# A decoder layer on one core: multiplications of a zero tile placed ahead of TensorE's waits in the first two bodies

## The reference: what is computed

```
x = layernorm(x + linear_attention(x))          # q, k = gelu(xW+b)+0.21, rotary; kv = k^T v per head, 16 heads of 8
x = layernorm(x + cross_attention(x, ctx))      # 77 context rows, softmax over them, output projection
x = layernorm(x + mixture_of_experts(x))        # 16 experts 128->256->128, top 4 of 16, all experts computed
```

## Time and profile before

| | before |
|---|---|
| runs | 711.3, 711.61, 710.29 us |
| median | 711.3 us |
| the profiled execution: its time | 711.3 us |
| the profiled execution: its span, first to last instruction | 709.5 us |
| PE busy | 640.7 us (90%), 6772 matmuls |
| VectorE, ScalarE, GpSimd busy | 433.1, 340.4, 107.8 us |
| mean granted TensorE clock | 0.991 |

### The profile page before, as it was taken

The page is one execution under the profiler, slowest core; times in us unless marked ns, Lnnn a source line. Parts: engine busy times, 40 slices in busy tenths (PEclk is TensorE's granted clock), DMA queues, the critical chain, the costliest instruction groups (busy, mean ns, idle before and its releaser), DMA issues.

```text
span 709.5 us, 17624 instructions
## 1 busy us (share of the span) xinstructions
PE 640.7 (90%) x6772; PEld 496.5 (70%) x6772; DVE 433.1 (61%) x1425; ACT 340.4 (48%) x439; POOL 107.8 (15%) x99
## 2 busy tenths in 40 slices
PE   1655886899999999999999999999999989999994
PEld 0433772678867887788778877887778766777773
DVE  0355455757588667867686758675876666356434
ACT  1511314276437643574438543864367435843440
POOL 6540200031002200221013000410032100000000
PEclk9999999999999999999999999999999999999998
DMA  7511001000010001010101000000100010000000
GB/s 195 153 31 46 18 11 37 18 3 27 16 39 18 18 15 47 2 30 9 37 18 30 9 24 28 17 24 12 40 17 0 4 34 4 17 1 1 16 1 16
DMA packets 27152, 19.17 MB, mean 27 GB/s; under 512 B 4568, under 2 KB 24776, under 8 KB 27112
## 3 DMA queue, kind: packets, MB, share of 16 engines
q1 hardware_dynamic: 22952, 13.39, 7.0%
q10 hardware_dynamic: 3872, 4.81, 2.2%
q0 software_dynamic: 288, 0.42, 0.2%
HBM read 8.85 MB, written 2.10 MB: 15 GB/s over the span
## 4 chain that ended last, share of the span: by engine, by line
PE 67%; issue 9%; SPq 9%; DVE 8%; ACT 2%; ACTq 2%; DMA 1%; POOL 1%; DVEq 0%; POOLq 0%
PE ps L792 25%; PE ps L743 9%; SPq L296 8%; PE ps L782 6%; PE ps L784 6%; PE ps L783 6%; PE ps L610 2%; DVE mx L985 2%; PE ps L635 1%; PE ps L624 1%; PE ps L706 1%; ACTq L454 1%; DMA q_rep<-zero_rows 1%; PE ps L629 1%; PE ps L720 1%
## 5 line engine op out<-in xcount | busy, mean ns | idle before, releaser
L792 PEld LDWEIGHTS ps<-w,g 128*128 128x128 f32 x2048 | 244.3, 192 | 25.2 <-issue 11.9
L792 PE MATMUL ps<-w,g 128*128 128x128 f32 x2048 | 256.0, 278 | 3.4 <-DVE acc L1086 3.2
L549 ACT ACTIVATE g<-ps,b 128x512 f32<-128x512 f32 x256 | 167.2, 685 | 162.5 <-PE ps L784 161.6
L1086 DVE SCALAR_TENSOR_TENSOR acc<-ps,cw,acc 128x128 f32<-128x128 f32 x448 | 126.1, 344 | 139.5 <-PE ps L792 139.4
L782 PE MATMUL ps<-x2h,w1h 128*128 128x512 f16 x256 | 98.0, 383 | 1.2 <-DVE x2l L1010 1.0
L784 PE MATMUL ps<-x2h,w1l 128*128 128x512 f16 x256 | 97.5, 381 | 0.0
L783 PE MATMUL ps<-x2l,w1h 128*128 128x512 f16 x256 | 97.5, 381 | 0.0
L374 POOL TENSOR_TENSOR rstd<-ve,half_pow 128x4 f32<-128x4 f32 x32 | 32.7, 1022 | 282.8 <-DVE ve L869 282.8
L524 ACT ACTIVATE w_stage<-ps 77x2048 f32<-77x2048 f32 x32 | 60.0, 1874 | 23.1 <-PE ps L720 22.9
L985 DVE TENSOR_REDUCE mx<-ps 128x8 f32<-128x616 f32 x64 | 49.0, 794 | 8.5 <-PE ps L706 7.5
L393 POOL TENSOR_TENSOR qr<-q_cos,q_sin 128x512 f32<-128x512 f32 x8 | 13.6, 1705 | 224.4 <-DVE q_sin L902 185.8
(11 more groups left out here) (146 smaller groups left out, 707.2 us busy)
## 6 DMA issues: line engine op xcount, KB each, us to landing
q_rep<-qx SPq DMA_DIRECT2D x96, 32.0 KB
x<-in_x SPq DMA_DIRECT2D x8, 256.0 KB, 2.9
w_stage<-in_L_ffn_w ACTq DMA_DIRECT2D x1, 2048.0 KB, 19.4
q_swap<-q SPq DMA_DIRECT2D x16, 128.0 KB, 2.0
out<-fin SPq DMA_DIRECT2D x8, 256.0 KB, 2.3
k_rep<-kx SPq DMA_DIRECT2D x96, 19.2 KB
cx<-in_ctx SPq DMA_DIRECT2D x8, 154.0 KB
cst<-constants ACTq DMA_DIRECT2D x1, 328.5 KB, 9.1
```

The source lines that it names most:

```text
L549: act.activation(g32[:, e % RING, h, :], bH[:, h, :], ACT.Gelu, bias=b1[:, e, h:h + 1], scale=1.0 / WS).then_inc(s["gelu"], 1)
L792: m = pe.matmul(bY[:, b * P:(b + 1) * P], g32[:, e % RING, h, b * P:(b + 1) * P], w2[:, e, h, :], start=(h == 0), stop=(h == HALF - 1))
L1086: m = dve.scalar_tensor_tensor(out=(acc_all if e == E - 1 else acc)[:, b, :], in0=bY[:, b * P:(b + 1) * P], scalar=cw[:, b, e:e + 1], in1= ...
```

## The change

A tile `idle` of zeros (128x512, f16) is added; VectorE writes it as its first instruction, and a semaphore `i_idle` tells PE. PE then issues 16 products of 128x128 by 128x512 of this tile into `bH` before its first real wait, and in the first two bodies `fill(name)` issues more of them ahead of the waits of the operations named in `FILL_FIRST` and `FILL_EARLY`. Each entry is a pair: so many long ones (512 columns) and so many short ones (128 columns). The results are never read. In all there are 66 long and 119 short ones. `filler` is empty from the third body on, and nothing else is changed.

```diff
+FILL_START = 16
+FILL_FIRST = dict(q=(14, 0), kv01=(0, 8), kv23=(0, 9), k_mean=(0, 12), kv=(4, 6), den=(0, 8), out=(0, 3), v1=(0, 5), k=(12, 0),
+                  x1_t=(4, 4), q_x=(0, 7))
+FILL_EARLY = dict(q=(0, 8), kv01=(0, 8), kv23=(0, 9), scores=(7, 0), max_t=(3, 3), kv=(0, 4), den=(0, 2), out=(0, 3), values=(0, 3),
+                  wo=(0, 5), q_x=(0, 7), x2_t=(6, 0), v1=(0, 5))
...
+        idle = sb("idle", [P, T], F16)
...
+            filler = {}
+
+            def fill(step):
+
+                long, short = filler.get(step, (0, 0))
+                for _ in range(long):
+                    pe.matmul(bH[:, 0, :], idle[:, 0:P], idle[:, :], start=True, stop=True)
+                for _ in range(short):
+                    pe.matmul(bH[:, 0, 0:P], idle[:, 0:P], idle[:, 0:P], start=True, stop=True)
+
+            pe.wait_ge(s["i_idle"], 1)
+            for _ in range(FILL_START):
+                pe.matmul(bH[:, 0, :], idle[:, 0:P], idle[:, :], start=True, stop=True)
             pe.wait_ge(s["ld_id"], 16)
...
                 if p == at["q"]:
+                    fill("q")
                     pe.wait_ge(s["i_wtc"], 2)
...
             def body(f, g, a):
-                nonlocal at
+                nonlocal at, filler
                 at = PE_EARLY if f is None else PE_AT
+                filler = {} if f is not None else FILL_EARLY if g is not None else FILL_FIRST
...
             at = DVE_EARLY
+            dve.memset(idle[:, :], 0.0).then_inc(s["i_idle"], 1)
```

More of the change, by code:

```diff
@@ L227, in build @@
         names = """ld_id ld_c ld_b1 ld_wide ld_xwide ld_xw ld_b ld_in ld_w1 ld_w2 ld_x ld_cx ld_swap ld_rep ld_mx st_out
-            i_ones i_idb i_rows i_wt i_wtc i_b1t i_b2 i_wh i_ws i_wl i_rw i_rwl i_v1 i_lg
+            i_ones i_idle i_idb i_rows i_wt i_wtc i_b1t i_b2 i_wh i_ws i_wl i_rw i_rwl i_v1 i_lg
             x_tp x_tc q_p qg q q_cos q_sin qr kv01_p kv23_p kb v kg k_cos k_sin kr
@@ L604, in linear @@
                     if p == at[("kv01", "kv23")[j]]:
+                        fill(("kv01", "kv23")[j])
                         if j == 0:
@@ L613, in linear @@
                 if p == at["k_mean"]:
+                    fill("k_mean")
                     since(pe, "kg", a + 1)
@@ L620, in linear @@
                 if p == at["kv"]:
+                    fill("kv")
                     since(pe, "kr", a + 1)
@@ L626, in linear @@
                 if p == at["den"]:
+                    fill("den")
                     since(pe, "kv", a + 1)
@@ L631, in linear @@
                 if p == at["out"]:
+                    fill("out")
                     since(pe, "den", a + 1)
@@ L647, in entry @@
                 if p == at["v1"]:
+                    fill("v1")
                     since(pe, "cx_tc", a + 1)
@@ L653, in entry @@
                 if p == at["x1_t"]:
+                    fill("x1_t")
                     since(pe, "x1", a + 1)
@@ L659, in entry @@
                 if p == at["k"]:
+                    fill("k")
                     since(pe, "v1", a + 1)
@@ L663, in entry @@
                 if p == at["q_x"]:
+                    fill("q_x")
                     since(pe, "x1_tc", a + 1)
@@ L669, in cross @@
                 if p == at["max_t"]:
+                    fill("max_t")
                     since(pe, "mxl", g + 1)
@@ L684, in cross @@
                 if p == at["wo"]:
+                    fill("wo")
                     since(pe, "ao", 2 * (g + 1))
@@ L689, in cross @@
                 if p == at["x2_t"]:
+                    fill("x2_t")
                     since(pe, "x2n", g + 1)
@@ L695, in scores @@
             def scores(g, b, half):
+                if b == 0 and half == 0:
+                    fill("scores")
                 if b == 0:
@@ L728, in values @@
                 M = 4 * HD
+                if b == 0:
+                    fill("values")
                 since(pe, "prob", n + 1)
```

## The result

| | before | after |
|---|---|---|
| runs | 710.29 to 711.74 us (4) | 718.9, 725.07, 722.55, 718.42 us |
| median | 711.45 us | 720.72 us |
| the profiled execution: time, span | 711.3, 709.5 us | 718.9, 717.1 us |
| instructions, all engines | 17624 | 17995 |
| mean granted TensorE clock | 0.991 | 0.951 |

The ratio is 1.0138, interval 1.0097 to 1.018. The change is slower, on the other side of the forecast and outside its range. The 371 further instructions are 185 products of two instructions each on PE (a weight load and a matmul) and the memset. The two mean clocks can't be held against each other: the kernel before shows 1.00 for its first 100 us, in which its products run at the low level, while the changed kernel shows its low stretches there (0.50 from 16 to 20 us).

A forecast was written before the change was run, and what follows sets the result against it. The chain of waits up to the second `kx` was taken as the bound, PE only after a second series of issues. Terms 3.1 + 1.0 + 0 + 1.0 = 5.1 us gave 711.3 - 5.1 = 706.2 us; 8-in-10 range 699.5 to 711.0.

The forecast's parts named there:

- whatever it gains up to there moves all that is behind it: Up to the second `kx`, at 107.02 us before: any gain there was taken to move everything later by as much.
- the slower side: Whole kernel slower by over 1.4 us, chance 0.07, given to fillers that last longer than the waits they stand in.
- The fillers' sum, 5.1 us: Total gain claimed: 3.1 first body, 1.0 second body's products, 0 values, 1.0 tail.
- `kg` 0.5 us earlier: First body, up to the gelu of k: gain 0.5 us, limited by ACT converting DMA-fed weights until 25.34 us.
- L624, L629, L635: 2.9, capped at 3.1 by POOL: First body: faster products gain 1.0 + 0.9 + 1.0, 3.4 us with the earlier 0.5, but POOL allows 3.1 at most.
- the rival of a fall before `kv`: First body: clock already falls before `kv`, L624, L629 and L635 stay slow; gain 1.5 us, 709.8 us, chance 0.18.
- L662 and scores low: L662 and the second body's scores come at the low clock level after long idle waits; no gain from either.
- Second body 1.0, values 0, tail 1.0: Gains taken from possible ranges: second body's products 0 to 2.8 us, values 0 to 7.0, tail 0 to 1.9.
- the first rival: Clock holds through the second body's values: gain 15.4 us, 695.9 us, or 700 with two fast; chance 0.20, some or all.
- Short filler 0.107 us, load nothing: Each short filler streams 0.107 us at the low level, 0.053 at the high; its weight load was taken as hidden.
- fillers outlast the waits: First two bodies: fillers finish after their waits and delay products, 712.1 to 714.2 us; chance 0.12 including no effect.
- that rival's streaming part: Streaming alone of fillers longer than their waits costs 0.8 us in all, second body's short waits counted.

The follow-up runs named there:

- pad_185: The kernel before with 185 one-column products at PE's start, the same 370 added instructions: 723.85 us against 711.29, ratio 1.0175.
- fill_pad_71: The changed kernel with all its fillers plus 71 one-column products at PE's start, a shift of 512 instructions: 710.86 us, ratio 0.9997 to the kernel before.
- more_fill: The changed kernel with longer fillers, more waits filled (values b=2 too) and 16 one-column products at the start, shift 512: 702.66 us against 712.1, ratio 0.9866.
- early_only: The changed kernel with only the start and second-body fillers, plus 39 one-column products, shift 256: 710.52 us, ratio 0.9976 to the kernel before.
- pad_2: The kernel before with 2 one-column products, a shift of 4 instructions: 718.38 us, one run.

## Why the prediction was wrong

**The step that failed** is in the first paragraph of the prediction: "whatever it gains up to there moves all that is behind it", with the sum that stops at the second `kx`. It takes the loop as a stretch that is only moved in time. It was also moved in the program, by 370 instructions, and that cost 12.6 us (`pad_185`), more than twice the whole forecast gain. No term of the sum and no rival stood for it, so the 0.07 of the slower side were given for another reason, and the range missed. The page before showed the ground for it: 27 packets of 16 KB are less than a loop of five passes would need if it were fetched in each. Both effects together, 723.85 - 0.4 = 723.5 us, lie within the 718.4 to 725.1 us measured; 720.7 is the median of only four, two at the high mean clock and two at the low.

**The fillers' sum, 5.1 us, measured 0.4** (from 711.29 to 710.86, interval -1.7 to +2.1 us of gain). Term by term:

- *`kg` 0.5 us earlier.* It came 1.85 us earlier (24.02 for 25.87). The bound was seen, ACT's conversion of weights that come by DMA, but taken as fixed; the DMA differs by 1.7 us between executions. In this one the conversion ended 1.3 us earlier (24.02 for 25.34), and what is left is the 0.5 forecast.
- *L624, L629, L635: 2.9, capped at 3.1 by POOL.* The residual sum is at 35.59 (predicted 35.4) and `kx` at 44.49 (44.3). That these came true is in part luck: about 1.3 us were the DMA, 1.2 to 1.6 the fillers. L624 stayed at 2.08, which the prediction had named as a sign against it; that is the rival of a fall before `kv`, in the first body, with a rise behind it that the rival did not have.
- *L662 and scores low*: right, 1.39 us, and 7.50 us idle where "3 us or more" was said.
- *Second body 1.0, values 0, tail 1.0.* The second `kx` came at 99.17 where 102 was said to be right. Two values ran at 1.08, which is half of the first rival. In `fill_pad_71` none did, and the stretch lost 0.7 us. One number for this part was the wrong form: in the profiled executions it has two outcomes, 4 to 5 us and about nothing. The wide spread of the runs fits that, and so do the mean clocks of the fastest runs. The rival's price was also added up a little high: four times 1.7 is 6.8 us, not 7.0, and 695.9 and two slow values give 699.3 us, not 700.
- *"the values, dense as they are, did not raise the clock, and I do not count on their holding it through the wait of 1.85 us ahead of b=2, which has no filler."* At that wait it fell, as the sentence has it. But b=0 and b=1 stand ahead of the wait, and the low stretch of before says nothing on whether such products stay high once the clock is. They do (1.08 us in both here, all four in `more_fill`). That they can't raise it isn't shown either: in the kernel before 7 us of them from 94.02 stayed low, and in `early_only` the clock rose while b=0 ran.
- *Short filler 0.107 us, load nothing.* In the chain it is 0.11 to 0.14 us at the low level, so the load is nearly hidden. The unhidden load of the Trainium skill's page "TensorE: Matmul & The Clock Gate", Part 2, LDWEIGHTS, is not seen; by that figure the two together would come to an estimated 0.21.
- *"fillers outlast the waits"*: the mechanism is real (0.43 us on the chain at `values`), its price under 1 us where the second body stayed low (0.7 in `fill_pad_71`), as that rival's streaming part had it. It did not decide the sign.
- *Spread wider than 1.3 us*: right, 6.7 us.

## What to carry to other kernels

A change ahead of a loop also moves the loop in the engine's program. Compare the packets of the instruction queue on the two pages, and look for a wait for `issue` behind the loop's branch back, before anything else is explained, and test an edit against a padding of the same number of instructions; then pad it to a whole block. Fill with zeros only where the wait is known to be long, fill every wait of the stretch to its end or expect the clock to fall at the one left out or just behind it (1.9 us idle ahead of b=2 were enough here), and read a gain of the first body against the landing of its DMA.

## What was not expected of the hardware

- A loop of 1781 PE instructions runs without a fetch or with nine 16 KB packets a pass, depending on where it begins: 711.3 us at shift 0, 718.4 at +4 (one pass fetches), 724.5 at +8 (three), 728.8 at +64, 723.9 at +114, and again 711.2 at +256. The stall stands behind the branch back.
- A fetch comes with a longer issue on another engine's queue. The chain of waits after, the last of the twelve issues to `k_rep` and the first to `q_rep` of the second spread:

```profile
106.71 0.59 SPq L303
107.30 0.04 issue
107.35 1.70 SPq L303
109.04 0.04 issue
```

One issue of SyncE takes 1.70 us in place of 0.59, at a time when the instruction queue has a packet under way; one in the first spread, at 53.28, takes 1.79, again with a packet. In the loop the twelve issues take 8.4 to 9.1 us for 7.5, and in `pad_2` 9.89 in the pass that refetches and 7.53 in the next. Of what the four passes lose, little can hang on it, since 12.0 us lie at the branch. The third body's lead fell from 7.85 us to 6.6 with one such issue in it.
- Zeros can raise the clock: nothing but zeros ran before 8.8 us, the first transposes then take 0.52 us in place of 0.88, and the 14 long fillers of `q` ran at 0.23 us each.
